# A one-element addition on GpSimd behind each gather of images 1 to 3

## The reference

```
samp = gather(y0, x0, ...) + gather(y0, x0 + 1, ...) + gather(y0 + 1, x0, ...) + gather(y0 + 1, x0 + 1, ...)
...
return jnp.einsum('ock,bckhw->bohw', weight.reshape(weight.shape[0], C, KK), samp)
```

## Time and profile before

| | |
|---|---|
| median of 3 runs | 770.78 us (753.77, 770.78, 781.69) |
| span of the profiled execution | 791.2 us; the page gives no other time for it |
| TensorE busy | 626.6 us, 79% of the span |
| VectorE busy | 439.6 us, 56% |
| ScalarE busy | 366.1 us, 46% |
| GpSimd busy | 363.9 us, 46% (288 gathers, 144 additions) |
| prologue with image 0 | from 0 to about 178 us |
| images 1 to 3: stretch with gathers, stretch without | 127.0 + 43.4 us, 132.4 + 42.7 us, 128.0 + 45.3 us |
| epilogue | from about 697 us to the end |

### The profile page before, as it was taken

How to read it: one execution, slowest core, us unless ns; L and a number is a source line. 1 busy time by engine, 2 the same in 40 slices (tenths; PEclk the granted TensorE clock), 3 DMA queues, 4 the chain that set the end, 5 groups by cost and what they waited for, 6 DMA issues and landing times.

```text
span 791.2 us, 9836 instructions
## 1 busy us (share of the span) xinstructions
PE 626.6 (79%) x2560; PEld 445.0 (56%) x2560; DVE 439.6 (56%) x1295; ACT 366.1 (46%) x762; POOL 363.9 (46%) x453
## 2 busy tenths in 40 slices
PE   6659776467976878994966958995869488999988
PEld 3445362127743656682744636683647366787766
DVE  2437469762885567453964547464848276444222
ACT  3125235642642456552543366552626175545442
POOL 1485665816486863035585852044778750000000
PEclk9977795767997979997987969996979879999999
DMA  8695894516255643165264632164465630400002
GB/s 309 194 307 193 319 310 118 150 36 200 68 163 160 175 134 115 41 212 161 70 186 133 174 115 82 68 205 138 113 179 144 199 109 25 138 9 1 0 1 106
DMA packets 46947, 109.94 MB, mean 139 GB/s; under 512 B 6575, under 2 KB 14831, under 8 KB 46778
## 3 DMA queue, kind: packets, MB, share of 16 engines
q0 software_dynamic: 23040, 75.52, 32.3%
q1 hardware_dynamic: 23866, 34.00, 12.6%
HBM read 96.94 MB, written 12.55 MB: 138 GB/s over the span
## 4 chain that ended last, share of the span: by engine, by line
PE 50%; another core or an unknown queue 14%; issue 12%; POOL 11%; ACT 6%; DVE 4%; DMA 3%; ACTq 0%; SPq 0%; DVEq 0%; POOLq 0%
PE bank L546 10%; PE bank L548 10%; PE bank L547 10%; POOL patch L514 9%; PE bank L701 6%; PE bank L665 4%; PE bank L563 3%; PE bank L691 2%; PE bank L711 2%; ACT ring L806 2%; POOL tick L512 2%; ACT samp L841 1%; DVE samp L1047 1%; DMA patch<-patch_tables,idx 1%
## 5 line engine op out<-in xcount | busy, mean ns | idle before, releaser
L1047 DVE SCALAR_TENSOR_TENSOR samp<-patch,wgt,samp 128x128 f32<-128x128 f32 x864 | 237.1, 346 | 92.1 <-ACT samp L841 58.5
L514 POOL DMA_INDIRECT patch<-patch_tables,idx x216 | 220.2, 1019 | 50.1 <-issue 36.3
L512 POOL TENSOR_TENSOR tick<-tick 1x1 f32<-1x1 f32 x144 | 60.9, 423 | 211.2 <-DVE wgt L1031 120.6
L701 PE MATMUL bank<-sampT,w 128*128 128x512 f32 x144 | 91.1, 719 | 44.8 <-ACT sampT L847 34.5
L841 ACT ACTIVATE samp<-patch,wgt 128x128 f32<-128x128 f32 x288 | 93.5, 392 | 24.7 <-DMA patch<-patch_table,idx 16.2
L691 PE MATMUL bank<-ident_r,samp 128*128 128x128 f32 x288 | 50.7, 299 | 48.1 <-DVE samp L1047 42.3
L514 POOL DMA_INDIRECT patch<-patch_table,idx x72 | 77.0, 1070 | 16.8 <-issue 12.0
L847 ACT ACTIVATE sampT<-bank 128x512 f32<-128x512 f32 x72 | 42.2, 587 | 83.5 <-remote 46.4
L1069 DVE TENSOR_TENSOR xs_low<-ring,xs_high 128x512 fp32r<-128x512 f32 x64 | 43.1, 689 | 66.3 <-ACT xs_high L810 48.8
L806 ACT ACTIVATE ring<-bank,prm 128x512 f32<-128x512 f32 x64 | 44.2, 701 | 77.0 <-PE bank L548 29.8
L691 PEld LDWEIGHTS bank<-ident_r,samp 128*128 128x128 f32 x288 | 38.3, 153 | 71.3 <-DVE samp L1047 56.3
(11 more groups left out here) (168 smaller groups left out, 1214.9 us busy)
## 6 DMA issues: line engine op xcount, KB each, us to landing
res<-in_x SPq DMA_DIRECT2D x32, 256.0 KB
out_y<-ring SPq DMA_DIRECT2D x32, 256.0 KB, 2.1
xa<-in_x SPq DMA_DIRECT2D x7, 1024.0 KB, 7.3
patch<-patch_tables,idx POOLq DMA_INDIRECT x216
patch_tables<-midT SPq DMA_DIRECT2D x11, 256.0 KB
patch<-patch_table,idx POOLq DMA_INDIRECT x72
xa<-in_x SPq DMA_DIRECT2D x4, 256.0 KB, 4.9
xa<-in_l1wt SPq DMA_DIRECT2D x1, 1024.0 KB
```

Source lines behind the costliest of these rows:

```text
L512: pool.tensor_tensor(tick[:, p:p + 1], tick[:, 0:1], tick[:, 0:1], ALU.add).then_inc(ticked, 1)
L514: pool.indirect_dma_start(patch[:, n % SLOTS].rearrange("p a c -> p (a c)"), None, table, bass.IndirectOffsetOnAxis(ap=idx[:, e:e + 1], ax ...
L701: pe.matmul(bank[6 + h][:], w2[:, k, :], sampT[:, u % 2, :], start=k == 0, stop=k == TAPS - 1).then_inc(tap_done, 1)
L1047: dve.scalar_tensor_tensor(o_, g_, w_, o_, ALU.mult, ALU.add).then_inc(blended, 1)
```

## The change

In images 1 to 3 each gather is followed by a one-element addition on GpSimd, line 519 of the changed kernel, on an element of `tick` of its own. It counts up a new semaphore, `paced`, which GpSimd alone waits for, at the start of an image. `tick` grows from 37 to 109 elements of one partition. Image 0 keeps its stream. No other engine's program changes.

```diff
-        tick = sb("tick", [1, 1 + 2 * UNITS])
+        tick = sb("tick", [1, 1 + 2 * UNITS + HT * UNITS])
...
                     pool.indirect_dma_start(patch[:, n % SLOTS].rearrange("p a c -> p (a c)"), None, table,
                                             bass.IndirectOffsetOnAxis(ap=idx[:, e:e + 1], axis=0))\
                         .then_inc(gathered[n % SLOTS], 16)
+                    if not isinstance(ib, int):
+                        q = 1 + 2 * UNITS + n
+                        pool.tensor_tensor(tick[:, q:q + 1], tick[:, 0:1], tick[:, 0:1], ALU.add).then_inc(paced, 1)
...
                         wait_past(pool, ticked, 2 * UNITS * ib)
+                        if not isinstance(ib, int):
+                            pool.wait_ge(paced, HT * UNITS * ic + 1)
...
+            pool.sem_inc(paced, 1)
             with pool.Fori(1, N) as i:
```

More of the change, by code:

```diff
@@ L332, in conv_seq_kernel @@
         tabled = [sem(f"tabled{u}") for u in range(2)]
-        taken, ticked = sem("taken"), sem("ticked")
+        taken, ticked, paced = sem("taken"), sem("ticked"), sem("paced")
         gathered = [sem(f"gathered{s}") for s in range(SLOTS)]
```

## The result

The changed kernel takes **717.94 us** (4 runs, 715.12 to 722.12), the kernel before on the same chip 772.83 us (4 runs, 753.77 to 781.69). The ratio is 0.948, with an interval of 0.941 to 0.955: 5% faster. A ratio compares only executions in the faster of two states, while the medians take in all of them, so it need not be the quotient of the medians (0.929 here). The profiled execution of the changed kernel took 718.57 us, with a span of 716.6 us.

A forecast was written before the change was run, and what follows sets the result against it. No single engine was taken to bound the kernel; loose time lay in starved stretches. GpSimd's 80 us of added work, a quarter on the path (+20), less 26 us of starving gave -6 us from 770.8: 765 us, range 715 to 815 us.

The forecast's parts named there:

- rival A: Gather stretches: wider spacing alone, 1.26 to 1.38 us, prevents all starving; -84 + 20 = -64 us, put at 720 us; chance 0.22.
- What bounds the kernel: Whole kernel: no single engine bounds it; TensorE idles 24 to 35 us in each gather stretch, mostly while starved.
- Pace, 23 us: GpSimd, images 1 to 3: additions delay the next gather, 4 us inside pairs and 19 us between; 7 to 40 us.
- Held additions, 57 us: GpSimd, images 1 to 3: VectorE holds the new additions as often as the old, 216 x 0.26 us.
- On the path: a quarter: GpSimd's 80 us of added work: a quarter lies on the chain, +20 us; waiting for slots covers the rest.
- Starved stretches, -26 us: Images 1 to 3: other engines starve during unbroken gathers, 84.0 us; more pauses of GpSimd win back 26 us.
- Against A: Inside a starved stretch: gathers 1.30 us apart, with an addition before them, did not prevent the starving.
- B: Gather stretches: GpSimd becomes the bound, its added work exceeding its waiting; +47 us, 818 us; chance 0.27.
- C: Gather stretches: additions vanish in GpSimd's 0.30 us idle time and starving stays; nothing changes, 771 us; chance 0.13.

The follow-up runs named there:

- image0_too: Changed kernel with the addition behind each gather of image 0 as well; 704.71 us, 1.032 of the kernel before, which took 683.87 us on that chip.
- in_pair_again: Changed kernel with only the 108 additions between the two gathers of a pair kept; 782.22 us, 1.001 of the kernel before (782.53 us).
- behind_pair: Changed kernel with only the 108 additions behind the second gather of a pair kept; 698.24 us, 1.020 of the kernel before (683.87 us).
- memset_every: Changed kernel with a one-element memset in place of the addition, behind every gather of all four images; 786.7 us, 1.000 of the kernel before (782.53 us).
- four_every_again: Changed kernel with four one-byte memsets in place of the addition, behind each gather of all four images; 738.82 us, 0.966 of the kernel before (766.83 us).

## Why the prediction went as it did

The forecast was 765 us, faster by less than can be measured; 717.94 us came, inside the range of 715 to 815 but only 3 us from its end, and it is rival A that came true, in its mechanism and at its 720 us. The mechanism of the forecast itself, which left two thirds of the starved time standing, did not. That A's 720 us was met to 2 us is partly luck: the 13 us by which it lay above A's own sum of 707 had no working.

- **What bounds the kernel.** Right: the loose time was in the starved stretches. The other engines recovered when GpSimd's gathers were spread.
- **Pace, 23 us.** Right. By the distances above it is 108 x 0.05 + 108 x 0.16 = 23 us. Between pairs two additions came 0.14 us apart, where I had taken 0.18, and inside a pair it was 0.05 us instead of 0.04.
- **Held additions, 57 us.** Wrong. The new ones took 262 ns, against 183 undisturbed, so 216 x 0.079 = 17 us. The old ones gave back 18 of their 28 us. Only 9 of the 216 took above 0.6 us. The longest took 2.34 us. The next is this one, at 208 us, where three subtractions of VectorE end together with it (timeline of POOL, then of DVE, kernel after):

```profile
208.32 1.99 POOL L519 TENSOR_TENSOR tick<-tick 1x1 f32<-1x1 f32 x1
```

```profile
208.38 1.89 DVE L1075 TENSOR_TENSOR xs_low<-ring,xs_high 128x512 fp32r<-128x512 f32 x3
```

  I had carried the mean of 108 additions over, which stood where GpSimd has just been waiting for VectorE's blends. The new ones stand elsewhere. The rule of the Trainium skill, "SBUF — State Buffer" (Who interferes with whom), that the shared ports are locked for a whole instruction, agrees in which additions are held: the 69 new ones that began while VectorE had no two-input instruction running took 0.18 to 0.19 us, all of them, and every longer one is among the 147 others. It does not tell how long: half of those 147 took 0.19 us or less, while the one at 208 us was held over three instructions and not one.
- **On the path: a quarter.** Wrong. Once nothing starves GpSimd bounds the gather stretches, and most of what it gets is paid: the calm chips show 14.4 of 17 us for the additions behind the pairs and 17.3 of 16.4 us for the memsets, though nothing for the additions inside the pairs. The errors in work and in share cancel, which is luck: 23 + 17 - 18 = 22 us of more work, and at most about 21 us of it paid (`image0_too` has the whole change and more, and costs 20.8), against my +20.
- **Starved stretches, -26 us.** This is the term that failed. I argued from the pauses of up to 3 us that more additions would bring, and took a bit more than the middle between nothing and -47. But the pauses were not the cure, the distance was: 108 more additions, 13 of them held, brought nothing in `in_pair_again`. All 84.0 us of the earlier trace rows went, the 13.8 us that I had put out of reach among them. The medians differ by 54.9 us, A's full relief was 64 (84 less 20). The two profiled spans differ by 74.6 us, but the one before lies 18 above the median of before.
- **Against A** I had put that gathers 1.30 us apart, inside a starved stretch, did not help. That was a true reading, and `in_pair_again` confirms it. It did not bear on 1.385 us, and I let it.
- **B.** Half of it holds: GpSimd did become the bound. Its sign depends on the chip. Where nothing starves, the half behind the pairs costs 2.0% and the memsets of the same mean distance 2.6%. The changed kernel itself did not run on a calm chip; from `behind_pair`'s 14.4 us and `image0_too`'s 20.8 us it would lose 2 to 3% there, an estimate.
- **C** holds for the kernels that hardly move the pace (`in_pair_again`, `memset_every`).

Open is what is starved and why only in some measurements. A gather's issue takes the 0.96 us of GpSimd on both kinds, and the traces name no releaser; the piece at 433.8 us of `memset_every` points to something that comes after the work of the engines, their signals or what follows them. Image 0, which still shows 12.46 us in the chain after, would gain by wider distances too, as `four_every_again` shows; with additions it was not measured on a starving chip, since `image0_too` met a calm one.

## What to carry to other kernels

Where several engines stand at once, with no releaser in the profile, and one engine goes on issuing the same thing, give that engine's pace a term of its own, and test distances step by step: no time was won up to 1.31 us, nearly all of it by 1.385. An added instruction costs at most what it moves the next one, which may be nothing (a 0.09 us memset) or its whole length (behind another addition). And time the kernel before on more than one chip before trusting either sign: the half behind the pairs is 5% faster on one and 2% slower on another.

## What was unexpected of the hardware

The same program took 681 to 684 us in two measurements and 767 to 783 us in four, on at least five chips. GpSimd's gathers, 0.96 us each and 1.26 to 1.32 us apart, kept ScalarE from going on for up to 15.1 us at a time on the slower kind, 13 us of them with TensorE and VectorE at a stand too. One tenth of a microsecond more between them on average, at which GpSimd was still busy for nine tenths of the stretch (99.08 of 110.90 us), ended it in images 1 to 3.
